# Distance bias scaled by GpSimd, layer-two weights in other buffers, and another order of VectorE's work between attention and ternary layer

## What is computed

```
x = x + tanh(g_xattn[0]) * attn0(layernorm(x), ctx)          # 16 heads of 16, no bias
x = x + tanh(g_ffn[0])   * ternary_ffn(layernorm(x))         # weights rounded to -s, 0, s; activations to 8 bits
x = x + tanh(g_xattn[1]) * attn1(layernorm(x), ctx, dist)    # scores + (-log(dist + 1e-9) * |scale|)
x = x + tanh(g_ffn[1])   * expert0(layernorm(x))             # relu(x w1 + b1) w2 + b2, then a layernorm
```

## Time and profile before

| | us |
|---|---|
| median of 3 runs (lowest, highest) | 387.9 (385.26, 388.23) |
| profiled execution: time | 389.54 |
| profiled execution: span | 387.8 |
| PE busy | 328.2 |
| DVE busy | 285.7 |
| ACT busy | 281.9 |
| POOL busy | 231.5 |
| mean granted clock of PE | 0.958 of full speed |

### The profile page before, as it was taken

How to read it: one execution, slowest core, us unless ns; L and a number is a source line. 1 busy time by engine, 2 the same in 40 slices (tenths; PEclk the granted TensorE clock), 3 DMA queues, 4 the chain that set the end, 5 groups by cost and what they waited for, 6 DMA issues and landing times.

```text
span 387.8 us, 8915 instructions
## 1 busy us (share of the span) xinstructions
PE 328.2 (85%) x3222; PEld 268.1 (69%) x3222; DVE 285.7 (74%) x684; ACT 281.9 (73%) x516; POOL 231.5 (60%) x405
## 2 busy tenths in 40 slices
PE   2877878887987587789778999999897999999992
PEld 2557668665855465467557898777786899888882
DVE  4977878776799999868785565788757548656667
ACT  4474799889898699998936788777679576555530
POOL 3575775777596332676777656755873286555442
PEclk9995799999899899969999999999999899999998
DMA  7698546101100005000182211222000000000001
GB/s 207 177 151 154 150 113 190 37 7 44 43 9 16 2 0 83 0 2 0 49 249 55 64 45 30 50 52 56 3 2 2 2 2 29 29 30 27 29 29 54
DMA packets 22963, 22.02 MB, mean 57 GB/s; under 512 B 4487, under 2 KB 22280, under 8 KB 22843
## 3 DMA queue, kind: packets, MB, share of 16 engines
q1 hardware_dynamic: 22920, 21.45, 23.1%
HBM read 10.34 MB, written 2.10 MB: 32 GB/s over the span
## 4 chain that ended last, share of the span: by engine, by line
PE 43%; ACT 24%; DVE 18%; issue 11%; POOL 2%; DMA 1%; ACTq 0%; SPq 0%; DVEq 0%; POOLq 0%
PE psA L1903 10%; PE psD L1887 5%; PE psA L1701 5%; PE psBE L1887 4%; PE psD L1610 3%; ACT pp_hi L777 3%; DVE mx L1239 3%; ACT p L768 3%; PE psBE L1636 2%; ACT wspace L848 2%; ACT space L833 2%; PE psA L1685 2%; DVE st L1004 2%; ACT xn L741 2%; ACT space L840 1%
## 5 line engine op out<-in xcount | busy, mean ns | idle before, releaser
L499 POOL TENSOR_TENSOR pp_lo<-p,pp_hi 124x512 f16<-124x512 f32 x80 | 96.9, 1232 | 39.0 <-ACT pp_hi L777 38.9
L1239 DVE TENSOR_REDUCE mx<-psBE 128x6 f32<-128x462 f32 (+1 forms) x96 | 54.5, 581 | 25.5 <-PE psBE L1636 25.1
L408 POOL TENSOR_TENSOR lns<-lns,mhalf 128x2 f32<-128x2 f32 x39 | 28.5, 732 | 71.7 <-DVE lns L1009 71.1
L768 ACT ACTIVATE p<-psD 124x512 f32<-124x512 f32 x80 | 47.6, 595 | 27.2 <-PE psD L1610 26.7
L1610 PE MATMUL psD<-qb,ktb 98*124 98x256 f16 (+1 forms) x256 | 48.7, 288 | 2.3 <-ACT p L768 1.8
L777 ACT ACTIVATE pp_hi<-p 124x512 f16<-124x512 f32 x80 | 50.4, 630 | 0.2
L1610 PEld LDWEIGHTS psD<-qb,ktb 98*124 98x124 f16 (+1 forms) x256 | 32.6, 144 | 7.3 <-ACT p L768 3.5
L1636 PE MATMUL psBE<-kt_hi,q_hi 128*128 128x154 f16 (+2 forms) x160 | 34.4, 284 | 3.0 <-ACT mT L759 2.1
L1330 DVE TENSOR_TENSOR pp_lo<-space,pp_hi 128x512 f16<-128x512 f32 x32 | 25.7, 822 | 13.6 <-ACT space L870 13.6
L1903 PE MATMUL psA<-ew_hi,pp_lo 128*128 128x256 f16 x128 | 34.9, 273 | 0.0
L1903 PE MATMUL psA<-ew_hi,pp_hi 128*128 128x256 f16 x128 | 34.9, 273 | 0.0
(11 more groups left out here) (214 smaller groups left out, 994.2 us busy)
## 6 DMA issues: line engine op xcount, KB each, us to landing
qb<-q_hi SPq DMA_DIRECT2D x32, 128.0 KB
xs<-in_x SPq DMA_DIRECT2D x8, 256.0 KB, 5.3
qb<-q_lo SPq DMA_DIRECT2D x16, 128.0 KB
tw_raw<-in_tw SPq DMA_DIRECT2D x2, 1024.0 KB, 5.6
space<-in_ew SPq DMA_DIRECT2D x2, 1024.0 KB, 7.4
out<-space SPq DMA_DIRECT2D x7, 256.0 KB, 2.1
ktb<-km SPq DMA_DIRECT2D x6, 248.0 KB, 5.4
qb<-bT_lo SPq DMA_DIRECT2D x8, 104.0 KB
```

Of the source, the lines that this page charges most:

```text
L499: nc.gpsimd.tensor_tensor(pl[:, u % 2, 2 * r:2 * r + 2, :], p32[:, n % 4, :, :], ph[:, u % 2, 2 * r:2 * r + 2, :], ALU.subtract).then_inc( ...
L768: a_(p32[:, n % 4, :, :], psD[n % 2][0:KR, :].rearrange("p (t r) -> p t r", t=2), ACT.Exp, scale=1.0 / SSC).then_inc(a["exp"], 1)
L1239: v.tensor_reduce(pairs[:, MP[k][0]:MP[k][1]:MP[k][2], :], psBE[:, n % 2, 0:hn * KEYS].rearrange("p (q e k) -> p q e k", e=2, k=KEYS), AX. ...
```

## The change

- The natural bias is scaled by GpSimd (`bias_natural`), ahead of its slots 6 and 7, with a new semaphore `s_bn`. ACT doesn't do it any more.
- The transposed distances are copied by a DMA into `distT2`, which lies over the first half of `tw_raw` (the raw tw1), after the log has been taken and tw1 has been rounded (`s_tw` 4). SP issues it between unit 7's query blocks and its `mT` row. GpSimd makes the high half from the copy (`bias_high`, two halves, in the drain), and DVE's two `bias_low` read the copy and stand later, among the ternary maxima of units 4 to 6.
- The first GELU waits for `s_bn` 2 and for the DMA instead of for both `bias_low`.
- The raw wo and wq of layer two are loaded into the buffers of layer one's wk and wv. SP waits for these two to be used first. ACT lays them out later: wq after the rounding of unit 5 (`weights_hi(1, "q")`), wo ahead of layer two's slot 0. DVE's `split_low` of wo goes behind layer two's slot 1, and PE waits for it at the first projection instead of at the first queries.
- DVE's drain begins with the statistics of unit 4. The roundings of tw2 number 0 to 2 follow, the keys (`split_keys`, `keys_high`) and the last rounding come behind the first ternary maxima, and the first two maxima stand right behind `divide(0, 6)`.

```diff
@@ (buffers)
+        wraw[1, "o"], wraw[1, "q"] = wraw[0, "k"], wraw[0, "v"]
+        distT2 = tw_raw[0:KEYS, 0, :]
@@ (SP)
             shift_rows(0, 3)
+            sp.wait_ge(s_wkp, 1)
+            sp.wait_ge(s_vp, 1)
             load_w(1, "qo")
             for u in range(4, NU):
                 query_blocks(0, u)
+                if u == NU - 1:
+                    sp.wait_ge(s_ln, 2)
+                    sp.wait_ge(s_tw, 4)
+                    sp.dma_start(distT2, distT[:, :]).then_inc(d_dT2, 16)
                 shift_rows(0, u)
@@ (POOL)
+            def bias_natural(i):
+                t = slice(i * NT // 2, (i + 1) * NT // 2)
+                pool.wait_ge(s_ln, 2)
+                pool.wait_ge(s_gsc, 3)
+                nc.gpsimd.tensor_tensor(bN[:, t, :], distN[:, t, :],
+                                        dcol[:, 0:1].unsqueeze(2).to_broadcast([128, NT // 2, KEYS]), ALU.mult).then_inc(s_bn, 1)
+            def bias_high(i):
+                c = slice(i * N // 2, (i + 1) * N // 2)
+                pool.wait_ge(d_dT2, 16)
+                nc.gpsimd.tensor_tensor(bT[0][:, c], distT2[:, c], dcol[0:KEYS, 0:1].to_broadcast([KEYS, N // 2]),
+                                        ALU.mult).then_inc(s_bt, 1)
...
             for s in range(NU):
+                if s in (6, 7):
+                    bias_natural(s - 6)
                 attn_slot(0, s)
...
             plo(0, 7, 4)
+            bias_high(0)
             factors_act(NU + 5, 1.0, A[0]["fac"])
+            bias_high(1)
             factors_act(NU + 6, 1.0, A[0]["fac"])
@@ (ACT, setup)
-                if s == 5 and r in (1, 4):
-                    act.wait_ge(s_ln, 2)
-                    act.wait_ge(s_gsc, 3)
-                    a_(bN[:, t, :], distN[:, t, :], ACT.Copy, scale=dcol[:, 0:1])
-                if s == 6 and r in (1, 4):
-                    a_(bT[0][:, c], distT[:, c], ACT.Copy, scale=dcol[0:KEYS, 0:1]).then_inc(s_bt, 1)
-                if s in (4, 5) and r == 3:
-                    weights_hi(1, "qo"[s - 4])
@@ (ACT, ternary stage)
                 if n == 0:
-                    act.wait_ge(s_bias, 2)
+                    act.wait_ge(s_bn, 2)
+                    act.wait_ge(d_dT2, 16)
...
             ternary_rounded(5, 1)
+            weights_hi(1, "q")
             ternary_transposed(4, 1)
...
+            weights_hi(1, "o")
             attn_slot(1, 0)
@@ (DVE)
-                if l == 0 and s == 7:
-                    bias_low(0)
...
-            bias_low(1)
+            residual_stats(0, 4, NU)
+            divide(0, 5)
             ternary_round(1, 0)
-            divide(0, 5)
-            split_low(1, wraw[1, "o"], whl[1, "o"])
             ternary_round(1, 1)
             ternary_round(1, 2)
-            ternary_round(1, 3)
-            residual_stats(0, 4, NU)
-            split_keys(1)
-            keys_high(1, 0)
             divide(0, 6)
             ternary_max(0, 0)
             ternary_max(0, 1)
             ternary_inverse(0)
             quantise(0, 4)
             residual(0, 5)
+            split_keys(1)
+            keys_high(1, 0)
             ternary_scale(0)
             keys_high(1, 1)
             residual_stats(0, 5, NU)
+            ternary_round(1, 3)
             divide(0, 7)
...
             ternary_scale(4)
+            bias_low(0)
             dve.wait_ge(A[0]["ppv"], 2 * NU)
             tables_v(1, 1)
...
             tables_v(1, 3)
+            bias_low(1)
             ternary_residual(3)
...
             attn_slot(1, 1, 3 * NU)
             keys_high(1, 3)
+            split_low(1, wraw[1, "o"], whl[1, "o"])
@@ (PE)
+                        if s == 3 and l == 1:
+                            pe.wait_ge(s_spl, 1)
                         project(l, s - 3)
...
                     if l == 1:
-                        pe.wait_ge(s_spl, 1)
                         pe.wait_ge(s_wqp, 2)
+                        pe.wait_ge(s_bn, 2)
```

More of the change, by code:

```diff
@@ L235, in build @@
         s_vop = sem("s_vop"); s_vo = sem("s_vo"); s_kt = sem("s_kt")
-        d_ktb = sem("d_ktb"); d_bb = sem("d_bb"); d_q = [sem(f"d_q{i}") for i in range(NQ)]
-        s_ln = sem("s_ln"); s_bt = sem("s_bt"); s_bm = sem("s_bm"); s_bias = sem("s_bias")
+        d_ktb = sem("d_ktb"); d_bb = sem("d_bb"); d_dT2 = sem("d_dT2"); d_q = [sem(f"d_q{i}") for i in range(NQ)]
+        s_ln = sem("s_ln"); s_bt = sem("s_bt"); s_bn = sem("s_bn"); s_bm = sem("s_bm"); s_bias = sem("s_bias")
         c_dve = sem("c_dve"); c_pool = sem("c_pool")
@@ L676, in setup @@
                     a_(gate[:, :], bc[:, 0:4], ACT.Tanh).then_inc(s_gate, 1)
-                t = slice(r // 3 * NT // 2, (r // 3 + 1) * NT // 2)
-                c = slice(r // 3 * N // 2, (r // 3 + 1) * N // 2)
                 if s == 3 and r == 3:
                     ternary_sum(0)
-                if s == 5 and r in (1, 4):
-                    act.wait_ge(s_ln, 2)
-                    act.wait_ge(s_gsc, 3)
-                    a_(bN[:, t, :], distN[:, t, :], ACT.Copy, scale=dcol[:, 0:1])
-                if s == 6 and r in (1, 4):
-                    a_(bT[0][:, c], distT[:, c], ACT.Copy, scale=dcol[0:KEYS, 0:1]).then_inc(s_bt, 1)
-                if s in (4, 5) and r == 3:
-                    weights_hi(1, "qo"[s - 4])
                 if s == 6 and r == 3:
@@ L1158, in bias_low @@
                 dve.wait_ge(s_bt, i + 1)
-                v.scalar_tensor_tensor(bT[1][:, c], distT[:, c], dcol[0:KEYS, 0:1], bT[0][:, c], ALU.mult,
+                v.scalar_tensor_tensor(bT[1][:, c], distT2[:, c], dcol[0:KEYS, 0:1], bT[0][:, c], ALU.mult,
                                        ALU.subtract).then_inc(s_bias, 1)
@@ L1320, in ternary_stats @@
                 dve.wait_ge(F["res"], u + 1)
+                ge(dve, F["xn"], u - 3)
                 stats(2 * NU + u, xs[:, 2 * u:2 * u + 2, :])
```

## The result

The changed kernel takes 384.65 us (median of 14 runs, 382.23 to 387.09), the kernel before 387.48 us (14 runs, 385.26 to 389.03). The ratio is 0.9934, 95% interval 0.9915 to 0.9953: faster by 2.6 us (1.8 to 3.3). The profiled execution of the changed kernel has a span of 383.2 us, against 387.8.

A forecast was written before the change was run, and what follows sets the result against it. It took extra ACT work to bound slots 5 and 6, DVE the drain, and ACT and DVE nearly full after it. Slots -2.8, drain -2.0 and low half +1.1 gave -3.7, so 384.2 us against the 387.9 median; range 379.8 to 388.6.

The forecast's parts named there:

- Slots, -2.8: Layer one's slots: without the moved ACT work, slots 5 and 6 shorten to an 11.0 us loop, gaining 0.8 and 2.0.
- rival A: Slots and drain: the loop isn't binding, ACT's time counts with 4.0 us, the drain gives 3.0; 380.9 us, chance 0.20.
- POOL's work, 0: Slots and drain: GpSimd's bias_natural (1.5 us) and bias_high (2.5 us each) fit its idle time and cost 0.
- the meeting that would have made the drain -1.0: Drain: split_keys on DVE could stand behind all of a bias_high on POOL, making the drain term -1.0.
- First rounding, -4.4: End of the drain: ACT's first rounding starts at 126.1 instead of 130.55 us, 4.4 earlier.
- Drain, -2.0: Drain and after: net gain 2.0 us (bounds -1.0 to -4.4), as DVE work moved behind the first maxima gives part back.
- ACT can't stay further ahead than about 2 us: After the drain: DVE is full there, so ACT's lead is limited to about 2 us; basis of the drain term.
- a new stretch of low clock: Sign that the prediction falls: a new stretch of low clock takes the gain; no size given.
- First low half, +1.1: Ternary stage: the first bias_low on DVE delays the copy at 166.30 us and PE's next table step, costing 1.1 us.
- wq, wo, `split_low`, second low half, queues, 0: Ternary stage and layer two: these moved pieces and the DMA and semaphore waits fall into idle time and cost 0.
- Rival B: Whole kernel: little is left, slots -1.5, drain -1.5, low half +1.5; 386.4 us, chance 0.30.
- Rival C: After 130 us: work moved behind the first maxima doesn't fit and the kernel gets slower; 392.2 us, chance 0.10.

The follow-up runs named there:

- e3_slot5_back: Changed kernel with natural bias, wq and wo all back on ACT in slots 4 and 5, no bias on POOL ahead of slots 6, 7; 385.32 us (one run).
- e4_slot6_back: Changed kernel with the high half of the transposed bias back on ACT in slot 6, none of it on POOL in the drain; 386.84 us (one run).
- e0_after: The changed kernel run once more without an edit; 384.87 us, ratio 0.9935 to the kernel before.
- e5_low_later: Changed kernel with the first bias_low moved behind the table copies, beside the second; 384.14 us, ratio 0.9912 to the kernel before.
- e2_fill_gap: Changed kernel with split_keys, the first keys_high and tw2's last rounding moved into DVE's gaps ahead of the first maxima; 382.98 us, ratio 0.9889 to the kernel before.
- e8_wq_slot4: Changed kernel with only ACT's wq layout back in slot 4; 385.08 us, ratio 0.9934 to the kernel before.
- e1_divide_early: Changed kernel with DVE's division of unit 7 put right behind split_keys; 384.7 us, ratio 0.9940 to the kernel before.

## Why the prediction was right, and where it wasn't

384.2 us was predicted, 384.65 measured; -3.7 us against -2.6 (1.8 to 3.3). The time came nearer than the gain, for with 14 runs the kernel before has a median of 387.48 and not 387.9. By its steps:

- **Slots, -2.8**: right, in mechanism and size. Slot 5 lost 0.81 (0.8 predicted), slot 6 lost 1.98 (2.0), slot 4 nothing. (Slot 4 took 11.81 us before, between the starts of `mT`, not 12.3.) e3_slot5_back and e4_slot6_back give each back alone. ACT's time didn't count in full, which was rival A: in the changed kernel it waits in slots 4, 5 and 7 for POOL's factors. Slot 7 gained 0.34 on top, with a granted clock of 1.00 where it was 0.85. That is luck: slot 5 of e0_after took as much more with the same low clock.
- **POOL's work, 0**: right. `bias_natural` took 1.21 us (1.5 estimated), `bias_high` 1.89 (2.5). The first `bias_high` was over at 121.7, ahead of `split_keys` at 123.4, so the meeting that would have made the drain -1.0 didn't happen.
- **First rounding, -4.4**: right, -4.34, and the wait of 3.49 us is gone.
- **Drain, -2.0**: too large. It was -0.5 in the trace shown and -1.3 in five others. The term rested on "ACT can't stay further ahead than about 2 us". The two numbers under it held: relative to the table load the division of unit 7 came 1.6 earlier (1.7 predicted) and unit 5's factors 2.6 earlier (3.0; though in the kernel before ACT has no idle time ahead of 137.30, so it didn't wait for them there). What failed is that PE was left out. It has transposes, the projection of unit 6 and the product of unit 0 in its order behind that division, and ACT waits for unit 4's rows behind them. PE came 1.7 us earlier to this work than before (13.29 against 14.97 us behind the table load), and it had been ready some 0.9 us before ACT then (141.67 against 142.55), so its 2.5 us of waiting need not have cost ACT anything. The low clock that came with the wait did: it made the same work 1.2 us longer in e0_after and 2.05 in the trace shown, and ACT waited 0.93 and 1.81. Without these waits the drain would be 19.3 us in both, -2.3, close to the -2.0. That is worked out from the rows and not run. The prediction named a new stretch of low clock only as a sign that it falls, and gave it no price.
- **First low half, +1.1**: the mechanism is right, the size too high. The copy of the tables lost 1.2 us of its lead (166.30 against 162.49, after 161.36 against 156.37 for the maximum before it), yet only 0.7 reached layer two (e5_low_later). That part of it fell into ACT's old wait of 1.27 is likely, not shown. The row was 1.78 us, where the second low half took 1.27 alone, and GpSimd's L555 beside it took 2.25 where it else takes 1.27 or 1.28: the two met as `keys_high` and `plo` do in e2_fill_gap.
- **wq, wo, `split_low`, second low half, queues, 0**: right as far as seen. wq was tried (e8_wq_slot4), wq and wo together in e3_slot5_back. `split_low` and the queues weren't tried alone; the last stretch of the table, 0.26 shorter, shows no cost.

That the sum came so near is in part luck. The drain fell 1.5 us short of its term in the trace shown and 0.7 in five others; 0.34 from slot 7's clock, 0.4 of too high a cost in the late stage and 0.26 in the last stretch stand against it. Rival B had the drain (-1.5) nearer and the slots (-1.5) wrong. Rival C, slower, didn't come about, though its mechanism did, in part: 2.8 us of moved DVE work, with the low clock that it led to, took some 2.4 of the 4.3 us back (e2_fill_gap).

## What to carry to other kernels

When an engine is relieved ahead of a wait and work is moved behind it, the gain that lasts is about the lead of the latest of the engines that meet next (and what slack it had there before), so follow the moved work to everyone who waits for what stands behind it, TensorE's in-order queue too. In e1_divide_early unit 5's factors led by 1.6 us and the drain gained 1.6; in e2_fill_gap they led by 3.7 and it gained 3.7. In the changed kernel it gained 1.3 or 0.5, less than any lead (1.6 to 2.6): there a wait of TensorE brought a low clock, which by the estimate above cost more than the wait. Before work is moved behind such a point, look for the gap that the relief itself opens: here DVE got 3.7 us of idle time ahead of the first maxima, and filling it was worth as much as two thirds of the whole change. An order that only moves a wait from one engine to another (e1_divide_early) is a hint that the amount of work in that stretch is the bound; it took e2_fill_gap, with work taken out of the stretch, to show it.

## What the runs showed of the hardware that wasn't expected

- The first 60 us, up to `mT` of slot 3, which no edit touches, differ by 3.4 us between the ten traces (58.49 to 61.89), and the last 197.5 us by 0.2 (197.40 to 197.56 in the changed kernel and its variants). Traces are better compared from an event behind the loads.
- The same idle time of PE (2.50 and 2.52 us) was followed by a granted clock of 0.50 over 4 us in one execution, and of 0.57 in another. PE came back to work at the same point in both (13.29 and 13.31 us behind the table load) and was through with it 0.9 us later in the first, and so the drain differs by 0.9 us.
